# Two cross attentions whose first three batches are sent in another order, with first loads in pieces

## The reference

```
x = x + cross0(layernorm(x), ctx, tau, delta)
x = x + block0(layernorm(x))     # self attention, then top-1 of 8 experts
x = x + cross1(layernorm(x), ctx, tau, delta)
x = x + block1(layernorm(x))     # permutation into expert sets and back

def cross(query, ctx, tau, delta):            # tau per batch, delta per key
    q = heads(query @ Wq.T + bq)
    k, v = heads(ctx @ Wk.T + bk), heads(ctx @ Wv.T + bv)
    scores = (q @ k.T * tau + delta) / 4
    return (softmax(scores) @ v) @ Wo.T + bo
```

## Time and profile before

| | |
|---|---|
| median of 3 runs | 963.87 us |
| profiled execution | 966.02 us, of it the span of the instructions 964.2 us |
| mean granted TensorE clock | 0.871 of full speed |
| PE busy | 786.9 us (82%) |
| DVE busy | 507.2 us (53%) |
| ACT busy | 344.5 us (36%) |
| POOL busy | 242.9 us (25%) |
| DMA | 103.29 MB, mean 107 GB/s |
| chain that ended last | PE 61%, DVE 13%, DMA 8%, ACT 5%, issue 5%, POOL 4%, SP's queue 4% |

### The profile page before, as it was taken

How to read it: one execution, slowest core, us unless ns; L and a number is a source line. 1 busy time by engine, 2 the same in 40 slices (tenths; PEclk the granted TensorE clock), 3 DMA queues, 4 the chain that set the end, 5 groups by cost and what they waited for, 6 DMA issues and landing times.

```text
span 964.2 us, 16230 instructions
## 1 busy us (share of the span) xinstructions
PE 786.9 (82%) x6103; PEld 597.1 (62%) x6103; DVE 507.2 (53%) x1223; ACT 344.5 (36%) x627; POOL 242.9 (25%) x242
## 2 busy tenths in 40 slices
PE   3557989899999999951499999956369898997898
PEld 3345666566666666531499999944246666675775
DVE  4544577876688676223112112224555788345495
ACT  2224544435354544510122222203124464443313
POOL 2422333322233231112211111014523442211100
PEclk9768988989999999965699999987677799755899
DMA  4949464754454665336544556425938252060202
GB/s 158 125 66 193 80 92 66 104 79 71 71 115 78 69 129 159 111 109 70 195 166 169 189 189 169 154 73 74 134 47 113 46 89 58 13 274 6 91 1 88
DMA packets 66896, 103.29 MB, mean 107 GB/s; under 512 B 21614, under 2 KB 56942, under 8 KB 61662
## 3 DMA queue, kind: packets, MB, share of 16 engines
q1 hardware_dynamic: 64403, 97.07, 47.9%
q0 software_dynamic: 2416, 5.19, 2.9%
HBM read 56.61 MB, written 7.28 MB: 66 GB/s over the span
## 4 chain that ended last, share of the span: by engine, by line
PE 61%; DVE 13%; DMA 8%; ACT 5%; issue 5%; POOL 4%; SPq 4%; DVEq 0%; POOLq 0%; ACTq 0%
PE PS L723 9%; PE U L734 8%; PE U L640 8%; PE MB L573 6%; PE MB L661 5%; PE PS L626 4%; PE MB L651 4%; PE MB L603 4%; DVE R L1262 3%; PE MB L589 3%; SPq L1459 2%; DMA y<-yb,pos 2%; DMA QKa<-mTa 2%; DVE nma L1071 2%; PE MB L813 2%
## 5 line engine op out<-in xcount | busy, mean ns | idle before, releaser
L1071 DVE TENSOR_REDUCE nma<-MB 128x2 f32<-128x512 f32 (+1 forms) x192 | 124.3, 673 | 43.9 <-PE MB L603 43.5
L899 ACT ACTIVATE Pa<-PS 128x1024 f32<-128x1024 f32 (+1 forms) x96 | 97.5, 1023 | 73.1 <-PE PS L626 72.1
L1304 POOL TENSOR_TENSOR mv<-mv,vec 128x2 f32<-128x2 f32 x48 | 34.7, 723 | 272.0 <-DVE mv L1026 271.8
L603 PE MATMUL MB<-QKa 99*128 99x120 bf16 (+1 forms) x512 | 75.1, 265 | 26.9 <-DVE nma L1071 14.2
L640 PE MATMUL U<-Pa,Vaa 128*32 128x256 f32 (+1 forms) x768 | 92.4, 405 | 0.9 <-ACT Pa L899 0.7
L723 PE MATMUL PS<-mzT,mw 128*128 128x128 f32 x736 | 87.8, 278 | 1.8 <-ACT mzT L920 1.8
L723 PEld LDWEIGHTS PS<-mzT,mw 128*128 128x128 f32 x736 | 85.7, 195 | 2.4 <-issue 2.3
L734 PE MATMUL U<-mw,mdT 128*128 x368 | 83.3, 379 | 2.3 <-DVE mdT L1210 2.3
L603 PEld LDWEIGHTS MB<-QKa 99*128 99x128 bf16 x512 | 41.3, 107 | 60.4 <-DVE nma L1071 22.1
L734 PEld LDWEIGHTS U<-mw,mdT 128*128 128x128 f32 x368 | 68.2, 190 | 11.0 <-issue 2.7
L1218 DVE TENSOR_TENSOR yt<-U,mb 128x256 f32<-128x256 f32 x23 | 9.8, 425 | 123.2 <-PE U L734 123.2
(11 more groups left out here) (194 smaller groups left out, 1424.6 us busy)
## 6 DMA issues: line engine op xcount, KB each, us to landing
mw<-in_mw SPq DMA_DIRECT2D x31, 1024.0 KB, 5.7
QKa<-spa SPq DMA_DIRECT2D x144, 128.0 KB, 5.2
Qb<-spb SPq DMA_DIRECT2D x48, 128.0 KB, 5.1
Oa<-Uba SPq DMA_DIRECT2D x16, 256.0 KB
v<-in_v SPq DMA_DIRECT2D x1, 4096.0 KB, 13.6
v<-in_v SPq DMA_DIRECT2D x4, 1024.0 KB, 11.4
W<-in_W SPq DMA_DIRECT2D x3, 1280.0 KB, 7.4
yb<-yt SPq DMA_DIRECT2D x23, 128.0 KB, 1.7
```

The costliest lines, as they stand in the source:

```text
L603: i = e.matmul(b[:, keys * j:keys * j + keys], Q[0:99, h0 + j, 128 * qt:128 * qt + 128], K[0:99, h0 + j, 0:keys], start=True, stop=True)
L899: e.activation(p[0:keys, :], ps[0:keys, :], ACT.Exp, scale=0.25).then_inc(sems["exp"], 1)
L1071: e.tensor_reduce(A.nm[qt][:, h0:h0 + heads], b[:, 0:heads * keys].rearrange("p (h s) -> p h s", h=heads), AX.X, ALU.max, negate=True).the ...
L1304: e.tensor_tensor(rs[r][:, 0:2], ve[r][:, 0:2], mhalf[:, 0:2], ALU.pow).then_inc(sems["rs"], 1)
```

## The change

The first steps of both cross attentions come in another order, the loads at the start are cut and spread, and two buffers get places of their own.

- Times: `EARLY` no longer shifts batch 1; keys of batch 2 (`EARLY_KEYS`) and the norm and queries of batches 1 and 2 (`T_EARLY`) have times of their own, as have the maxima of batches 1 and 2 (`T_MAX_EARLY`) and the values of the first three batches (`T_VALUES`). Both pipelines with cross attentions use these tables.
- Loads: keys' weights, queries' weights and the small vector table are issued by ACT; the rest of the weights, and `ctx` past its first two batches, follow later on SP. `x` of batches 3 to 7 is one step of five DMAs.
- `dr`, `dr1` and `dsp` (the parts of `delta`) lie at the end of their area instead of in the buffers of the splits, and ACT's wait for `dsx` is gone.
- The fill of the values' ones (`Vaa`, a step `va` now) comes later.

```diff
-EARLY = (0, 0.213, 0.9)
+EARLY = (0, 0, 0.9)
+EARLY_KEYS = (0, 0, 2.6)
+T_EARLY = ((-2.75, -2.55, -2.35, -2.3, -2.2, -2.1), (-2.0, -1.85, -0.7, -0.5, -0.1, 0.1))
 T_MAX = ((-1.75, -0.312), (-1.57, -0.55), (-1.75, -0.312))
+T_MAX_EARLY = ((-1.2, -0.3), (-1.25, -0.3))
+T_VALUES = -1.2
...
-T_LOADS = (-3.2, -1.5, -0.5, 0.5, 1.0, 1.6)
+T_LOADS = (-1.95, 1.0, 1.6)
...
-                task(at(T_KEYS[L]), [("kp", n)], [("ks", n)], [("kr", n), ("kd", n)])
-            task(at(T_KEYS[L][1:]), [("vp", n)])
-            task(at(T_CROSS), [("na", n, 0)], [("nb", n, 0)], [("zt", n)], [("qp", n)], [("qs", n)], [("qd", n), ("of", n)])
+                task(at(T_KEYS[L], EARLY_KEYS), [("kp", n)], [("ks", n)], [("kr", n), ("kd", n)])
+            task(at((T_VALUES if m < 3 else T_KEYS[L][1],)), [("vp", n)])
+            task(T_EARLY[m - 1] if m in (1, 2) else at(T_CROSS), [("na", n, 0)], [("nb", n, 0)], [("zt", n)], [("qp", n)], [("qs", n)], [("qd", n), ("of", n)])
...
+        ((-2.0,), [[("va", 0)]]),
-    out += [("a2",), ("tb", 2), ("wc",)]
-    others = [([(EARLY[b] if b < 3 else b) + t for t in T_BEFORE], [[("bg", b)], [("ba", b)]]) for b in range(NB)]
+    out += [("a2",), ("va", 2), ("tb", 2), ("wc",)]
+    others = [([-4.8, (-3.95, -2.77, -2.05)[b]] if b < 3 else [b + t for t in T_BEFORE], [[("bg", b)], [("ba", b)]]) for b in range(NB)]
...
-            self.dr, self.dr1 = self.tq[0][0:8, 0, 0:CK], self.tq[1][0:8, 0, 0:CK]
-            self.dsp = self.sp3[0][0:8, :, 0, 0:CK]
+            d = Area(s.p - 4096, s.p)
+            self.dr, self.dr1 = (d.new(f"dr{tag}_{i}", [128, CK])[64:72, :] for i in range(2))
+            self.dsp = d.new(f"dsp{tag}", [128, 3, CK], BF)[64:72, :, :]
...
-            g.wait_ge(f"d_dsx_{tag(n)}", 48)
...
+        def first_loads(_):
+            for piece, cols in (("k", slice(512, 1024)), ("q", slice(0, 512))):
+                e.dma_start(LW[0].all[:, cols], D["W0"][:, cols]).then_inc(sems[f"d_W0{piece}"], 16)
+            e.dma_start(vec[:, 0:133], D["vec"]).then_inc(sems["d_vec"], 16)
...
         def first_loads(_):
-            e.dma_start(vec[:, 0:133], D["vec"]).then_inc(sems["d_vec"], 16)
+            e.dma_start(AA.dr, D["delta"]).then_inc(sems["d_delta_a"], 16)
             load_x(0)
+            e.dma_start(AA.ctx[:, :, 0:CK2], D["ctx"][:, :, 0:CK2]).then_inc(sems["d_ctx_a0"], 16)
             e.dma_start(idf[:, :], D["idf"]).then_inc(sems["d_idf"], 16)
-            load_weights(0)
...
         def first_attention():
-            attention_loads(AA, "a", 4)
+            delta_rows(AA, "a", 4)
             load_x(1)
+            stack_rows(AA, "a")
+            e.dma_start(LW[0].all[:, 1024:2560], D["W0"][:, 1024:2560]).then_inc(sems["d_W0"], 16)
+            load_x(2)
+            e.dma_start(AA.ctx[:, :, CK2:], D["ctx"][:, :, CK2:]).then_inc(sems["d_ctx_a1"], 16)
+            e.dma_start(AA.sel[:, :, :, :], D["sel"]).then_inc(sems["d_sel_a"], 16)
...
-            if i < 4:
-                load_x(i + 2)
-            elif i == 4:
-                load_x(6)
-                load_x(7)
+            if i == 0:
+                for t in range(3, 8):
+                    load_x(t)
+            elif i == 1:
```

More of the change, by code:

```diff
@@ L74, in pipeline, with at @@
         m, L = n - first, layer(n)
-        e = EARLY[m] if m < 3 else m
-        def at(times):
-            return [(e if times[0] < -2 else m) + t for t in times]
+        def at(times, early=EARLY):
+            return [(early[m] if m < 3 and times[0] < -2 else m) + t for t in times]
         if cross(n):
             if n % 2 == 0:
-                task(at(T_KEYS[L]), [("kp", n)], [("ks", n)], [("kr", n), ("kd", n)])
-            task(at(T_KEYS[L][1:]), [("vp", n)])
-            task(at(T_CROSS), [("na", n, 0)], [("nb", n, 0)], [("zt", n)], [("qp", n)], [("qs", n)], [("qd", n), ("of", n)])
+                task(at(T_KEYS[L], EARLY_KEYS), [("kp", n)], [("ks", n)], [("kr", n), ("kd", n)])
+            task(at((T_VALUES if m < 3 else T_KEYS[L][1],)), [("vp", n)])
+            task(T_EARLY[m - 1] if m in (1, 2) else at(T_CROSS), [("na", n, 0)], [("nb", n, 0)], [("zt", n)], [("qp", n)], [("qs", n)], [("qd", n), ("of", n)])
         else:
@@ L93, in pipeline @@
         segments += [[("mh", n, 1)], [("mt", n)]]
-        task(at(even(2 * per + 3, *T_MAX[L])), *segments)
+        task(at(even(2 * per + 3, *(T_MAX_EARLY[m - 1] if m in (1, 2) and L != 1 else T_MAX[L]))), *segments)
         task(at(T_PROJECT[L]), [("p0", n)], [("p1", n)], [("p2", n)])
@@ L136, in order @@
     out += pipeline(0, 16, [
-        (T_LOADS, [[("ld", i)] for i in range(6)]),
+        ((-2.0,), [[("va", 0)]]),
+        (T_LOADS, [[("ld", i)] for i in range(3)]),
         ((NB + 2.5,), [[("w3",)]]),
@@ L480, in build @@
     names += [f"d_w1{i}" for i in range(3)]
-    names += ["d_o0", "d_o1"] + [f"d_{w}_{t}" for w in ("delta", "ctx", "ones", "dsx", "sel") for t in "ab"]
+    names += ["d_o0", "d_o1"] + [f"d_{w}_{t}" for w in ("delta", "ones", "dsx", "sel") for t in "ab"]
+    names += ["d_W0q", "d_W0k", "d_ctx_a0", "d_ctx_a1", "d_ctx_b"]
     sems = {name: stack.enter_context(nc.semaphore(f"s_{name}")) for name in names}
@@ L511, in landed, with loaded, context @@
         return f"d_{what}{n % 4}", {"q": 96, "m": 16}[what] * (n // 4 + 1)
+    def loaded(what, n):
+        return f"d_W{layer(n)}{what if n < 8 and what in 'qk' else ''}", 16
+    def context(n):
+        return ("d_ctx_b" if n >= 16 else "d_ctx_a0" if n < 2 else "d_ctx_a1"), 16
     def keys_of(n):
@@ L568, in project_in @@
                 g.wait_ge("z_turned", z_of(n) + 1)
-            g.wait_ge(f"d_W{layer(n)}", 16)
+            g.wait_ge(*loaded(what[0], n))
             g.free(BANKS.free[what, n])
@@ L975, in turn @@
                              ACT.Identity).then_inc(sems["turned_a"], 1)
-        does = {"zt": z_turn, "qp": lambda n: project_in("qp", n), "kp": lambda n: project_in("kp", n), "mt": max_turn,
+        def first_loads(_):
+            for piece, cols in (("k", slice(512, 1024)), ("q", slice(0, 512))):
+                e.dma_start(LW[0].all[:, cols], D["W0"][:, cols]).then_inc(sems[f"d_W0{piece}"], 16)
+            e.dma_start(vec[:, 0:133], D["vec"]).then_inc(sems["d_vec"], 16)
+        does = {"in": first_loads, "zt": z_turn, "qp": lambda n: project_in("qp", n),
+                "kp": lambda n: project_in("kp", n), "mt": max_turn,
                 "sc": scores, "pv": values, "gt": gate_turn, "ro": tile_in, "be": tile_turn,
@@ L985, in vector, with value_ones, delta_parts @@
         g = Gate(e, sems)
-        def copy_in(_):
-            g.wait_ge("d_idf", 16)
-            e.tensor_copy(idb[:, :], idf[:, :]).then_inc(sems["idb"], 1)
-        def ones_and_delta(A, t):
-            for i in range(4):
-                e.memset(A.Va[i][:, :, :, 1:32:2], 1.0).then_inc(sems["va"], 1)
+        def value_ones(L):
+            if L == 0:
+                g.wait_ge("d_idf", 16)
+                e.tensor_copy(idb[:, :], idf[:, :]).then_inc(sems["idb"], 1)
+            for v in att(8 * L).Va:
+                e.memset(v[:, :, :, 1:32:2], 1.0).then_inc(sems["va"], 1)
+        def delta_parts(A, t):
             k = 0 if t == "a" else 4
@@ L1274, in combine @@
             e.tensor_tensor(x[:, t, :], x[:, t, :], pair("cm", t)[:, 0:256], ALU.add).then_inc(sems["added"], 1)
-        does = {"in": copy_in, "a0": lambda: ones_and_delta(AA, "a"), "a2": second_attention, "tb": query_bias,
+        does = {"va": value_ones, "a0": lambda: delta_parts(AA, "a"), "a2": second_attention, "tb": query_bias,
                 "na": norm_stats, "nb": norm_apply, "qs": lambda n: split_mid("qp", n), "ks": lambda n: split_mid("kp", n),
@@ L1294, in loads @@
         def loads(i):
-            if i == 5:
+            if i == 2:
                 e.memset(y[:, 0, 0:128], 0.0).then_inc(sems["y0"], 1)
@@ L1429, in second_attention @@
             g.wait_ge("own", 6)
-            attention_loads(AB, "b", 8)
-        def loads(i):
-            if i < 4:
-                load_x(i + 2)
-            elif i == 4:
-                load_x(6)
-                load_x(7)
+            e.dma_start(AB.dr, D["delta"]).then_inc(sems["d_delta_b"], 16)
+            e.dma_start(AB.ctx[:, :, :], D["ctx"]).then_inc(sems["d_ctx_b"], 16)
+            stack_rows(AB, "b")
+            delta_rows(AB, "b", 8)
+            e.dma_start(AB.sel[:, :, :, :], D["sel"]).then_inc(sems["d_sel_b"], 16)
+        def loads(i):
+            if i == 0:
+                for t in range(3, 8):
+                    load_x(t)
+            elif i == 1:
                 e.dma_start(gw[:, :, :], D["gw"]).then_inc(sems["d_gw"], 16)
```

17 lines of the change are left out of this document (7 added, 10 removed).

## The result

| | before | changed |
|---|---|---|
| median of 20 runs | 965.2 us | 971.83 us |
| ratio, 95% interval | | 1.0052 [1.003, 1.0074] |
| profiled execution, its span | 966.02, 964.2 us | 972.34, 970.5 us |
| mean granted clock | 0.871 | 0.865 |

A forecast was written before the change was run, and what follows sets the result against it. It took the DMA engines as busiest in both cross attentions' starts, the maxima's rows queueing behind sends. -5.5 and +1.5 us sum to -4.0: 966.0 becomes 962.0 profiled, 959.9 beside the median of 963.9; range 948 to 970.

The forecast's parts named there:

- The first projection and ACT's first copy: Kernel start, fewer loads ahead: first projection at 5.4 us, not 11.96; ACT's first copy at 10.4, not 17.04.
- Start of the maxima: First cross attention: DVE's first reduction 20.6 us behind ACT's first copy plus added DVE work, at 33.1, 4.6 earlier.
- First scores: First cross attention: maxima's rows issued at 45.2 us, landing in 3.6; first scores at 48.8, not 58.57, 9.8 earlier.
- Batch 2 pays: First cross attention: batch 2's later sends put its maxima at 65.4 us, PE idles 4.8; of 9.8 gained, 0.4 is left.
- To the first sums: First cross attention, from batch 2's maxima: 19.9 us, not 18.6, with +3 for half clock; reaches 85.3, 1.0 later.
- What comes back: From there to batch 4's maxima: `Oa`'s wait (3.2) and half clock (4.5) fall away; 10.0 us, at 95.3, 5.5 earlier.
- The second cross attention: Its start: first scores at 701.8 us, not 704.25, but batch 20's keys later, at 724.3 and faster; 1.5 us lost.
- Batch 2 starves PE: Rival, chance 0.14: maxima of batches 2 and 18 come 8 us later, PE's waits cost more; 978, one stage alone 969.
- The gap closes: Rival, chance 0.24: batch 2's sends land before PE runs out of work at 60.6 us, in both cross attentions; 946.
- It does nothing: Rival, chance 0.07: the gain at the start is used up by 84 us and `Oa` isn't earlier; 964 to 965.

The follow-up runs named there:

- late_only: The changed kernel with the rest of `ctx` and the table `sel` issued behind batch 1's sends in the first cross attention; ratio 1.0051 to the kernel before.
- norm1: The changed kernel with the norm of batches 1 and 17 ahead of the split of the first keys again; ratio 1.0047 to the kernel before.
- best: sends0 with later `x`, second half of `ctx` and `sel` behind batch 1's sends, batch 2's norm behind the split of batch 0's queries; ratio 0.9929.
- second_old: The changed kernel with the order of the kernel before put back in the second cross attention alone; ratio 0.9981 to the kernel before.
- sends0: Old order, loads in pieces, values of batches 0 and 1 behind batch 1's queries, batch 2's twelve sends behind the first maxima's rows; ratio 0.9969.
- sends02: sends0 with batch 18's sends also behind the first maxima's rows in the second cross attention; ratio 0.9882 to the kernel before.

## Why the prediction was wrong

*The first projection and ACT's first copy* were forecast at 5.4 and 10.4 us (the sums as written give 5.3 and 10.3) and came at 6.08 and 10.74. Right.

*Start of the maxima* failed. The 20.6 us from ACT's first copy to DVE's first reduction were taken over from the kernel before; the first reduction came at 36.07 and not 33.1. That length was no constant: it held a chain that the change made longer. Two things now end there within 1.2 us of each other, batch 0's sends behind 2.4 MB of loads issued from 6 to 10 us (34.88), and DVE's work in order (36.07), which starts late with the norm of batch 1. Each taken away alone gains nothing (late_only, norm1, the latter with a last send that lands late); with the loads, batch 2's norm and its wait for `x` out of the way in the old order the first maxima come at 31.42 (best). The prediction saw that norm stand behind a split in the second attention, and not in the first.

*First scores* and *Batch 2 pays* were sized rightly but began late: the rows landed in 2.1 us (forecast 3.6), the first scores at 51.09 (48.8), batch 2's maxima 15.0 us behind the first send (15.1), at 68.39 (65.4). PE idled 3.4 us ahead of them and not 4.8, as its own work was late too (65.0 and not 60.6).

*To the first sums*: 21.05 us from there to the last scores of batch 1, forecast 19.9. *What comes back* failed by 3.5 us: 13.5 and not 10.0. The wait for `Oa` is gone, as said, and the new wait for batch 4's queries didn't come, but the half clock stayed: the sums took 3.67 us (3.54 in the earlier trace rows), at a granted clock of 0.50 from 90 to 100 us. Waits on ACT's copies and on DVE's split of the maxima of 1.2 to 1.7 us each, five of them between 60 and 88 us, stand ahead of it; that they brought the clock down is likely and not shown. The Trainium skill's rule that a loss is paid at each gap (TensorE: Matmul & The Clock Gate, "HAM oscillation — how this bites in real kernels") was used for the one gap put in; there the trace agrees, as the values behind it took 2.02 us (70.02) and 1.12 later on (78.97). In sum, batch 4's maxima are 2.1 us late (0.9 early in second_old) and not 5.5 early.

*The second cross attention* is the step that decided: "1.5 us lost" measured 7.6. Two of its terms failed. The first scores were to come 2.4 us earlier and came 0.1 later: the gather was taken to land at 691 for want of other sends, and that its issue stands behind batch 17's late split was not followed to its end, though the text had that norm 4 us late. In norm1, with that norm early again, the first scores come 5.7 us earlier. And the keys of batch 20 at full clock were to give 1.3 us back. They ran in 1.92 us (2.3 forecast), but the gain was lost behind them: from them to the sums it took 16.2 us, and 14.1 before, with the sums at 3.67 (2.22 before). The first term is 2.6 of the 6.1 us by which the step was off, the second 3.4. The way from first scores to those keys was right: 22.6 us, forecast 22.5.

*The rivals.* "Batch 2 starves PE" named 2.0 us as its deciding point; batch 2's and (counted from the keys of batch 16) batch 18's maxima were 3.0 and 2.9 us later than forecast, and 971.8 lies in its 969 to 978. It had a chance of 0.14, too little, since each step's lateness goes into the next and the sum had taken each at its best. Its mechanism did not come with its number: PE's waits ahead of those maxima, 3.4 and 2.1 us, were shorter than forecast and not longer. "The gap closes" fell. "It does nothing" was right that the gain at the start is used up by 84 us (the last scores of batch 1 are at 89.44, and at 84.34 before), and wrong on the time.

That the first attention's 2.1 us show in no ratio is no riddle: the same order gave 102.97 and 99.95 for batch 4's maxima, and the stretch behind varies by 5 us. Why norm1's 4.9 us in the second attention show in no ratio stays open.

## What to carry to other kernels

When transfers crowd out a wait, move the transfers and leave the work that makes them where it fills idle time: twelve issues moved alone won 8.2 us (sends0 to sends02) in the stage in which the change, which moved the whole batch and batch 17's norm, lost 7.6. Ahead of a forecast, follow what each late step has behind it on every in-order engine up to the one that issues the next transfer. And an earlier start was worth little here until every wait between it and the bound was shorter too. There were four: values ahead of the queries that waited for weights, batch 2's norm that waited for `x`, loads ahead of the sends, and batch 2's sends ahead of the maxima's rows.
